# Where the linear half of a mixture's up-projection gets its bias and its clip

## The reference, cut to what matters

```python
p1 = einsum('bsh,eoh->bseo', nf, mlp1_weight) + mlp1_bias
g = minimum(p1[..., 0::2], LIMIT)              # gate half, LIMIT = 7
lin = clip(p1[..., 1::2], -LIMIT, LIMIT)       # linear half
act = g * sigmoid(ALPHA * g) * (lin + 1.0)
p2 = einsum('bsei,ehi->bseh', act, mlp2_weight) + mlp2_bias
combined = einsum('bseh,bse->bsh', p2, combine)
```

## Time and profile before

| | |
|---|---|
| median of 3 runs | 2142.7 us (2140.57 to 2145.62) |
| span of the profiled execution | 2140.0 us |
| busy over the span | PE 94%, PEld 79%, DVE 65%, ACT 49%, POOL 45% |
| mixture stage | about 905 to 1265 us |
| one full step of it (six of them) | 37.7 us |
| granted PE clock over the span | 0.97 of full |

### The profile page before, as it was taken

The page is one execution under the profiler, slowest core; times in us unless marked ns, Lnnn a source line. Parts: engine busy times, 40 slices in busy tenths (PEclk is TensorE's granted clock), DMA queues, the critical chain, the costliest instruction groups (busy, mean ns, idle before and its releaser), DMA issues.

```text
span 2140.0 us, 54537 instructions
## 1 busy us (share of the span) xinstructions
PE 2005.3 (94%) x22465; PEld 1680.3 (79%) x22465; DVE 1390.1 (65%) x3108; ACT 1046.5 (49%) x2108; POOL 972.0 (45%) x762
## 2 busy tenths in 40 slices
PE   7999999999999999869999689999999999989994
PEld 4677777777777777658888679999999999988883
DVE  6766676767676766457888675555566455456983
ACT  3666666666666665414545443343244234224551
POOL 1555555555555555415554343433433443344441
PEclk9999999999999999979999889999999999999996
DMA  7001020101010101131230120000121100030000
GB/s 273 6 19 51 18 102 11 55 11 55 11 55 13 48 11 39 40 125 42 69 114 11 50 85 12 13 13 12 55 67 52 32 18 17 17 125 25 12 16 15
DMA packets 59991, 97.16 MB, mean 45 GB/s; under 512 B 7721, under 2 KB 50481, under 8 KB 57393
## 3 DMA queue, kind: packets, MB, share of 16 engines
q1 hardware_dynamic: 57184, 86.69, 12.2%
q10 hardware_dynamic: 2560, 6.99, 0.9%
HBM read 70.45 MB, written 23.20 MB: 44 GB/s over the span
## 4 chain that ended last, share of the span: by engine, by line
PE 41%; DVE 7%; issue 4%; ACT 2%; POOL 2%; DMA 1%; SPq 0%; DVEq 0%; POOLq 0%; ACTq 0%
PE psum L262 13%; PE psum L273 10%; PE psum L1992 4%; PE psum L1980 2%; PE psum L243 2%; PE psum L1966 2%; PE psum L2484 2%; PE psum L1336 1%; DVE b_act L1557 1%; PE psum L1323 1%; PE psum L2518 1%; PE psum L222 1%; ACT e_pr L2623 1%; DVE b_acc L1565 1%; POOL b_act_lo L1476 1%
## 5 line engine op out<-in xcount | busy, mean ns | idle before, releaser
L768 POOL TENSOR_TENSOR a_sm<-a_sm,a_rsum 128x1024 f32<-128x1024 f32 x256 | 479.8, 1893 | 384.7 <-DVE a_rsum L802 382.7
L790 DVE CUSTOM_DVE_ANT_0 a_sm<-psum,a_strip 128x1024 f32<-128x1024 f32 x256 | 312.1, 1219 | 147.3 <-PE psum L623 147.3
L704 ACT ACTIVATE a_sm<-a_sm,a_mn 128x1024 f32<-128x1024 f32 x256 | 293.9, 1148 | 30.0 <-DVE a_mn L790 28.8
L709 ACT ACTIVATE a_pT<-psum 128x512 f32<-128x512 f32 x256 | 151.6, 592 | 270.6 <-PE psum L636 270.6
L636 PE MATMUL psum<-ident,a_sm 128*128 128x128 f32 x2048 | 274.7, 277 | 3.7 <-POOL a_sm L768 2.4
L636 PEld LDWEIGHTS psum<-ident,a_sm 128*128 128x128 f32 x2048 | 224.0, 141 | 60.0 <-issue 45.1
L651 PE MATMUL psum<-a_pT,a_V 128*64 128x256 f32 x2048 | 250.6, 387 | 0.6 <-ACT a_o L715 0.6
L651 PEld LDWEIGHTS psum<-a_pT,a_V 128*64 128x64 f32 x2048 | 136.7, 137 | 78.1 <-issue 23.3
L797 DVE COPY a_pT<-psum 128x512 f32<-128x512 f32 x256 | 174.9, 683 | 10.9 <-PE psum L636 3.6
L2076 ACT ACTIVATE g_val<-psum 128x512 f32<-128x512 f32 x64 | 38.1, 597 | 216.7 <-PE psum L1992 216.7
L1476 POOL TENSOR_TENSOR b_act_lo<-b_act,b_act_hi 128x512 fp32r<-128x512 f32 x64 | 90.5, 1419 | 103.2 <-ACT b_act_hi L1374 103.2
(11 more groups left out here) (355 smaller groups left out, 4221.3 us busy)
## 6 DMA issues: line engine op xcount, KB each, us to landing
a_strip<-table SPq DMA_DIRECT2D x16, 960.0 KB, 6.5
oT<-a_o SPq DMA_DIRECT2D x64, 128.0 KB, 1.9
b_oT_in<-oT SPq DMA_DIRECT2D x8, 1024.0 KB, 5.5
a_raw<-in_a_wqkv SPq DMA_DIRECT2D x7, 384.0 KB, 3.3
s_x<-in_x_rev SPq DMA_DIRECT2D x4, 512.0 KB, 7.4
vb<-s_zero SPq DMA_DIRECT2D x8, 256.0 KB, 2.9
b_x_in<-in_x SPq DMA_DIRECT2D x8, 256.0 KB, 5.6
b_vb_in<-vb SPq DMA_DIRECT2D x8, 256.0 KB, 5.5
```

The source lines that it names most:

```text
L704: a.activation(sm[:, st % RING, :], sm[:, st % RING, :], ACT.Exp, scale=-1.0, bias=mn[:, at:at + 1], accum_out=rsum[:, at:at + 1]).then_in ...
L709: a.activation(probs(st, 0), psum[:, 4, :].rearrange("p (k q) -> p k q", k=4), ACT.Copy).then_inc(sig("pT_act"), 1)
L768: g.tensor_tensor(sm[:, st % RING, :], sm[:, st % RING, :], rsum[:, at:at + 1].broadcast_to([P, T]), ALU.mult).then_inc(sig("scaled"), 1)
L790: v.tensor_tensor_reduce(out=sm[:, st % RING, :], in0=scores_banks(hl).rearrange("p c n -> p (c n)"), in1=strip[:, pair % 2, hl, qt * P:qt ...
```

## The change

PE's bias products and all that served them (b1r, pick, their fills, the transpose, the semaphores ones, br_ps, br_out) are taken out. ACT's `gated` also waits for the linear half's bank and copies it with Identity and a bias (bias + 1, made once by DVE), in two instructions of 128x256, into `lin`; that copy now frees the bank. DVE's `clipped` waits for ACT's copy and clips `lin` in place in SBUF. No call is moved.

```diff
-    NB, ONE = E0 * KC, 32
-    b1l, b1r, pick = sb("b1l", [P, NB]), sb("b1r", [P, P], BF16), sb("pick", [P, NB, CP], BF16)
+    b1l = sb("b1l", [P, E0, KC])
...
-        if s == 0:
-            units += [(sig, "br", 0)]
...
         def up(s, e):
             pe.wait_ge(have("w1"), 16)
-            pe.wait_ge(sig("ones"), 4)
-            pe.wait_ge(sig("br_out"), 1)
...
                     for k in range(KC):
                         last = pe.matmul(half, w1[:, k, at:at + P], nT[:, s % 2, k, :],
-                                         start=k == 0, stop=part == 0 and k == KC - 1)
-                    if part:
-                        last = pe.matmul(half, b1r[:, :], pick[:, e * KC + m, :], start=False, stop=True)
+                                         start=k == 0, stop=k == KC - 1)
...
-            if s == 0:
-                pe.wait_ge(sig("wide"), 1)
-                pe.transpose(banks.take(pe, "br", 0)[0:NB, 0:P], b1l[:, :], ident[:, :]).then_inc(sig("br_ps"), 1)
...
             last.then_inc(sig("ug_out"), 1)
+            a.wait_ge(sig("ul_ps"), n + 1)
+            for m in range(KC):
+                last = a.activation(lin[:, n % ER, m, :], banks("ul", n)[:, m * CP:(m + 1) * CP],
+                                    ACT.Identity, bias=b1l[:, e, m:m + 1])
+            last.then_inc(sig("ul_out"), 1)
...
         def clipped(s, e):
             n = s * E0 + e
-            v.wait_ge(sig("ul_ps"), n + 1)
-            if n >= ER:
-                v.wait_ge(sig("m_act"), n - ER + 1)
-            v.tensor_scalar(lin[:, n % ER, :, :], halves(banks("ul", n)), LIMIT + 1.0, 1.0 - LIMIT,
-                            ALU.min, ALU.max).then_inc(sig("ul_out"), 1)
+            v.wait_ge(sig("ul_out"), n + 1)
+            v.tensor_scalar(lin[:, n % ER, :, :], lin[:, n % ER, :, :], LIMIT + 1.0, 1.0 - LIMIT,
+                            ALU.min, ALU.max).then_inc(sig("ul_clip"), 1)
...
             v.wait_ge(sig("ug_out"), n + 1)
-            v.wait_ge(sig("ul_out"), n + 1)
+            v.wait_ge(sig("ul_clip"), n + 1)
...
-            if s == 1:
-                v.wait_ge(sig("ones"), 1)
-                v.wait_ge(sig("br_ps"), 1)
-                v.tensor_copy(b1r[0:NB, :], banks("br", 0)[0:NB, 0:P]).then_inc(sig("br_out"), 1)
...
-                v.tensor_copy(b1l[:, :].rearrange("p (e k) -> p e k", e=E0), b1b[:, :, 1, :])
+                v.tensor_scalar(b1l[:, :, :], b1b[:, :, 1, :], 1.0, None, ALU.add)
                 v.tensor_copy(w2[:, :, :, :], w2b[:, :, :, :]).then_inc(sig("wide"), 1)
-                v.memset(b1r[:, :], 0.0).then_inc(sig("ones"), 1)
-                v.tensor_copy(pick[:, :, :], ident[:, 0:NB].rearrange("p (n o) -> p n o", o=1).broadcast_to([P, NB, CP])).then_inc(sig("ones"), 1)
-                v.wait_ge(sig("ones"), 2)
-                v.memset(b1r[ONE:ONE + 1, :], 1.0).then_inc(sig("ones"), 1)
-                v.memset(pick[ONE:ONE + 1, :, :], 1.0).then_inc(sig("ones"), 1)
```

More of the change, by code:

```diff
@@ L916, in mixture_early @@
     sig.reserve("ay_out ay_ps bT_hi bT_out bT_ps b_exp b_inv b_probs bn_eps bn_h bn_rstd bn_stats bn_var bp_out bp_ps bq_out bq_ps "
-                "br_out br_ps bs_out bs_ps bv_hi bv_out bv_ps by_out by_ps ld0 ld1 m2_out m2_ps mT_out mT_ps m_act m_combine m_exp "
+                "bs_out bs_ps bv_hi bv_out bv_ps by_out by_ps ld0 ld1 m2_out m2_ps mT_out mT_ps m_act m_combine m_exp "
                 "m_gap m_hi m_lo m_ms m_normed m_out m_rms m_ss mb_out mb_ps mc_out mc_ps mg_out mg_ps mn_eps mn_h mn_rstd "
-                "mn_stats mn_var ones st0 st1 ug_out ug_ps ul_out ul_ps v_chain w_hi w_lo wide x1_bo x3 x_bo")
+                "mn_stats mn_var st0 st1 ug_out ug_ps ul_clip ul_out ul_ps v_chain w_hi w_lo wide x1_bo x3 x_bo")
     early["have"].reserve("wo bias wq bwo gate rows0")
```

## The result

The changed kernel takes 2196.03 us (median of four runs, 2192.64 to 2196.64) against 2141.64 us of the kernel before, run beside it (2138.82 to 2145.62). The ratio is 1.0252, with a 95% interval of 1.0237 to 1.0267. The forecast was 2195 us.

What follows compares the result with a forecast made beforehand. DVE's in-order list bounds x1 to by and PE the rest of each step; 42 us of full-step waits, 4.5 for steps 8 and 9 and 6 for the clock add 52.5 to 2142.7: 2195 us, range 2162 to 2222.

Steps and rivals of the forecast that it cites:

- The bound: From x1 to by (22.61 us) DVE's list sets the time; in the other 15.11 us of a step PE does.
- What leaves: 128 bias matmuls, 14 us of PE time; only 0.65 us a step, 5.2 us over 8 tiles, lies in the PE-bound part.
- The stalls: DVE waits for ACT's copies at clips 3 to 7: 6.95 us from x1 to by, a full step 7.0 us longer.
- part of it is given back: Rival: delays behind the stalls of clips 3 and 5 vanish; a step grows by 4 us, 2170 us, chance 0.15.
- The clip: On DVE a clip takes 0.43 us from SBUF against 684 ns from PSUM, a gain of 0.25 us each.
- The clock: PE's granted clock falls behind gaps ahead of bT, bp and by: 1.0 us a full step, 6 in all.
- The full steps: Six full steps of the mixture, s = 2 to 7, each 7.0 us longer from waits: 42 us, plus 6 for the clock.
- steps 8 and 9: The mixture's last steps: 2.5 us at clipped 5 and 1 elsewhere in step 8, 1 in step 9; together 4.5.
- The sum: 42 + 4.5 + 6 = 52.5 us on top of 2142.7, giving 2195 us.
- The waits were not hidden: Rival: ACT reaches each pair early enough, so the waits are hidden; faster, 2136 us, chance 0.06.
- table load: Rival: Identity needs another table than the gelu, loads of 1.28 us at 64 copies and back; 2310 us, chance 0.02.
- The long fall of the clock: Rival: two clock falls a step on the path and a clip at 684 ns; 80 us more, 2222 us, chance 0.14.

Runs made afterwards that it cites:

- the gaps filled: The changed kernel with 20 useless matmuls on TensorE ahead of its wait for bT and 22 ahead of bp, in steps 2 to 7: 2180.09 us.
- before, clips late: The kernel before with clips 3, 5, 6 and 7 moved later in VectorE's list, clip still from PSUM, bias products kept: 2138.89 us, ratio 0.9999.
- before, copies alone: The kernel before with two more ScalarE Identity instructions behind each gelu pair, from SBUF to a tile nobody reads: 2146.89 us, ratio 1.0034.
- clip 3 moved: The changed kernel with only clip 3 moved, from ahead of the norm h to behind it: 2182.90 us, ratio 1.0188.
- the copies first: The changed kernel with ScalarE's copy of the linear half ahead of each expert's gelu instead of behind it: 2150.91 us, ratio 1.0052.
- limits per partition: The changed kernel with copies ahead of gelus and clips 3, 5, 6, 7 moved later, clip limits read from an SBUF tile instead of constants: 2150.96 us.
- all clips late: The changed kernel with every clip moved in VectorE's list to directly ahead of the product that uses it: 2144.39 us, ratio 1.0021.

## Why the prediction was right, point by point

**The bound.** That the stretch from x1 to by is DVE's list, and that the attention rides on it, held. One clip moved by a few places in that list is worth 2.4 or 3.3 us a step, with its part of the clock, and 128 matmuls taken off TensorE were worth 0.84.

**What leaves.** The 0.65 us of the PE-bound part was exact in the kernel before. In the changed kernel the part from by to x1 took 15.65 us in place of 15.11, where I had forecast 0 with bounds of -0.65 and +0.9. The clip of expert 2 waits 2.15 us just ahead of x1, as worked out, and the clip of expert 0 took 1.21 us beside GpSimd, which was not in the sum. That these two make the 0.54 is my reading; no run takes them apart.

**The stalls, the heart of the sum.** My working puts the wait at gelu start + 1.6 less the clip's old start. Place by place, forecast wait and measured wait in the step shown:

| clip | forecast | measured |
|---|---|---|
| 3 | 2.3 | 1.80 |
| 4 | 0.6 | 0.51 |
| 5 | 3.15 | 3.37 |
| 6 | 0.95 | 0.64 |
| 7 | 1.75 | 1.60 |
| sum | 8.75 | 7.92 |

In three of the five steps clip 6 waits 1.43 us, with the clock low. After what the shorter clips and the freed product give back, I had 6.95 us from x1 to by; with the clock at 1.00 throughout it was 6.31, in the kernel with the gaps filled. The product behind clip 7's wait took 0.68 us as forecast, where it was 1.27. The delays add up, since ScalarE gets as late as DVE: the gelu of expert 7 started 19.62 us behind x1 and starts 25.57 us behind it in the step shown (1088.71). The rival that part of it is given back did not come about.

**The clip.** 0.43 us was the right value where it runs alone, and the mean is 0.515, since a few take 1.2 to 1.3. That is 0.085 x 8 = 0.7 us a step on DVE's list that the sum didn't have, nearly all of it in the clip of expert 0.

**The clock, the term that was mis-sized.** I took 1.0 us a step from the 0.57 in the earlier trace rows, with bounds of 0 and 3.4. Measured were 1.84. I had argued that TensorE sets the time in only half the places where a fall can hit. But the two gaps stand ahead of bT (2.27 us) and bp (2.39), and after each of them TensorE does work that DVE or ScalarE waits for. It is 5 us too little over six steps. The Trainium skill (TensorE: Matmul & The Clock Gate, HAM oscillation) tells of a clock that falls again in every round behind a long idle wait. The steps here do the same, 0.84, 1.00, 0.85 and 1.00 in the one shown, but behind shorter gaps than the page names, 2.26 to 2.70 us; the trace decides.

**The full steps, then steps 8 and 9.** For the six full steps I had 42 + 6 = 48 us; up to the last x2 it was 52.4, and the clock's 5 us are the larger part of what is missing. For steps 8 and 9 the forecast was 4.5, measured 5.5 (57.9 - 52.4).

**The sum.** The forecast for the mixture was 52.5 us, and it was 57.9 at the start of the next stage's norm. The profiled span grew by only 50.8 (2190.8 - 2140.0), so some 7 us came back behind the mixture, and that is why the total of 2195 fits the median of 2196.03 better than its terms deserve: that close a fit is luck. I can't name a cause for it. Over the other eleven kernels the same difference (change in span less the delay at that norm, against before) runs from -7.3 us (before, clips late) to +5.2 (before, copies alone), in kernels that don't differ behind the mixture. So it is more likely a spread of the single profiled runs than an effect of the change; the profiled execution of after is the fastest of its four, 3.4 us under their median, and the medians of after and before differ by 54.4 us, which leaves 3.5.

**The rivals.** The waits were not hidden. No table load stands ahead of any copy. The long fall of the clock was partly there: two falls in a step, though they cost 1.84 us on average and not 3.4.

**What the change could have been.** No version of it beat the kernel before. Its possible gain on TensorE, 0.84 us a step, stands against 0.54 for ScalarE's copies, and against the time for which clips and products stand still beside GpSimd.

## What to carry to other kernels

Before an operand moves to an engine that has it later, take for every reader the producer's new end less the reader's old start in its in-order list; that sum, not the busy times, was right here to 10% (6.95 us against 6.31). It counts for what is queued behind the reader: with clip 3 moved, DVE idled as long and the step was 2.40 us shorter. If the move is wanted anyway, put the reader directly ahead of its own user (49 of 54 us came back here), or the new producer ahead of its slower neighbour and of any table load (44 of 54). A gap in TensorE's list that comes back in every step can cost more than itself: gaps of 2.3 to 2.7 us here brought the clock down, 1.84 of 8.47 us a step, and with the copies first, where the longest was 1.53 us, it stayed at 1.00.

## What the runs showed of the hardware

**A clip in SBUF can be held off by GpSimd, one from PSUM wasn't.** All 64 clips from PSUM in the kernel before took between 657 and 692 ns, also where GpSimd was at work first, as beside the clip at 1050.71 (0.68 us) of the earlier trace rows:

```profile
1049.89 1.28 POOL L1476 TENSOR_TENSOR b_act_lo<-b_act,b_act_hi 128x512 fp32r<-128x512 f32 x1 [0.21 <-ACT b_act_hi L1374]
```

The same operation in SBUF took 393 to 1299 ns in the changed kernel (median 427), and those of 0.6 us and more end a quarter of a microsecond after an operation of GpSimd that began before them: 1099.77 + 1.21 = 1100.98, and 1099.54 + 1.16 = 1100.70 for GpSimd's:

```profile
1099.54 1.16 POOL L1515 TENSOR_TENSOR b_x<-b_x,b_mo 128x512 f32<-128x512 f32 x1 [2.27 <-DVE b_mo L1567]
```

The Trainium skill (SBUF — State Buffer, Who interferes with whom) states that a `tensor_scalar` in a two-port mode shares a port pair with GpSimd, and that the later of the two blocks fully; these rows agree. It also states that an operation with at most one SBUF input outside such a mode doesn't contend, and the clips from PSUM agree. The kernel with limits per partition is no test of that, since at 514 ns and more its clip seems to be in the fast mode still.

**A shorter operation ahead of one that is held off can gain nothing.** In the kernel with all clips late, 1.9 us a step off the clips came back as 2.2 us in the products behind them: three of the eight in a full step (in one step a fourth, of 1.78 us) take 1.57 or 1.58 us and end 0.54 to 0.56 us after GpSimd's operation.
